# First layer's loads reordered, the last butterfly stage made as two products per tile, and a token table with 16 words per place

## The reference

```python
sim = einsum('bhnd,bhmd->bnm', Q, K) / (sqrt(d) * H)      # Q, K from the context
threshold = top_k(sim, 153)[0][:, :, -1:]
A = sigmoid(sim) * (sim >= threshold)
A = (A + swapaxes(A, -1, -2)) * 0.5
x = x + tanh(g_xattn[0]) * ((1 - gamma) * layernorm(x) + gamma * A)

hidden = silu(up_gate) * up_lin                            # (b, s, 2048)
hidden = fwht(hidden)                                      # 11 butterfly stages, / sqrt(2048)
x = x + tanh(g_ffn[0]) * einsum('bsh,dh->bsd', hidden, W2)
```

```python
topk_vals, topk_idx = top_k(xf @ router_w.T, 2)
order = argsort(topk_idx.reshape(-1))
x_sorted = xf[order // 2]
```

## Time and profile before

| what | us |
|---|---|
| median of 3 runs | 3995.62 |
| profiled execution, its own time | 4001.03 |
| its span (first to last instruction) | 3999.2 |
| PE busy | 3661.6 (92%) |
| DVE busy | 1982.6 (50%) |
| ACT busy | 1377.6 (34%) |
| POOL busy | 355.7 (9%) |

### The profile page before, as it was taken

How to read it: one execution, slowest core, us unless ns; L and a number is a source line. 1 busy time by engine, 2 the same in 40 slices (tenths; PEclk the granted TensorE clock), 3 DMA queues, 4 the chain that set the end, 5 groups by cost and what they waited for, 6 DMA issues and landing times.

```text
span 3999.2 us, 35714 instructions
## 1 busy us (share of the span) xinstructions
PE 3661.6 (92%) x11789; PEld 1695.6 (42%) x11790; DVE 1982.6 (50%) x3587; ACT 1377.6 (34%) x2838; POOL 355.7 (9%) x380
## 2 busy tenths in 40 slices
PE   1999999986789999599879999999999999999999
PEld 0444444432445444356534444444444434444443
DVE  8556666145678776211156756656565652111111
ACT  5524242011357667122233443434343441100100
POOL 7000000000123231211111100000000000000000
PEclk6999999998889999799989999999999999999999
DMA  3321312300322322455532101010101102222221
GB/s 119 126 79 54 132 57 75 112 23 22 86 69 62 74 59 82 156 162 160 170 133 67 50 32 36 24 36 24 36 24 36 36 1 84 85 78 79 84 84 52
DMA packets 78347, 295.90 MB, mean 74 GB/s; under 512 B 10856, under 2 KB 11752, under 8 KB 66684
## 3 DMA queue, kind: packets, MB, share of 16 engines
q1 hardware_dynamic: 69856, 268.35, 21.0%
q0 software_dynamic: 8352, 25.78, 2.1%
HBM read 255.73 MB, written 33.64 MB: 72 GB/s over the span
## 4 chain that ended last, share of the span: by engine, by line
PE 79%; DVE 8%; issue 7%; ACT 3%; DMA 2%; POOL 1%; SPq 0%; DVEq 0%; POOLq 0%; ACTq 0%
PE BM L2293 6%; PE BM L2348 5%; PE BM L529 5%; PE BR L529 5%; PE BR L2357 4%; PE BM L364 4%; PE BR L364 4%; PE BS L2331 3%; PE BS L545 3%; PE BT L545 3%; PE BT L2340 3%; PE BM L2306 3%; PE BR L1989 3%; PE BM L1978 2%; PE BR L1978 2%
## 5 line engine op out<-in xcount | busy, mean ns | idle before, releaser
L2422 ACT ACTIVATE AR<-BS,AR 128x512 f32<-128x512 f32 x256 | 174.5, 685 | 411.5 <-DVE AR L2517 411.5
L2416 ACT COPY AR<-BM 128x512 f32<-128x512 f32 x340 | 198.8, 585 | 307.2 <-PE BM L2348 99.9
L2530 DVE SCALAR_TENSOR_TENSOR X<-BR,AR,X 128x512 f32<-128x512 f32 x256 | 191.9, 750 | 206.2 <-PE BR L2357 197.1
L2517 DVE TENSOR_REDUCE AR<-BS 128x2 f32<-128x1024 f32 x128 | 156.9, 1226 | 253.8 <-PE BS L2331 253.8
L2357 PE MATMUL BR<-AR 128*128 128x512 f32 x512 | 254.8, 621 | 4.2 <-DVE X L2530 0.6
L2348 PE MATMUL BM<-AR 128*128 128x512 f32 x512 | 246.7, 594 | 0.0
L2293 PE MATMUL BM<-XT,AR 128*128 128x512 f32 x512 | 236.6, 605 | 0.7 <-ACT XT L239 0.7
L364 PE MATMUL BM<-XT,AR 128*128 (+1 forms) x512 | 231.7, 595 | 4.9 <-DMA AR<-l_w_dram 4.9
L419 DVE TENSOR_TENSOR AR<-AR,BR 128x512 f32<-128x512 f32 x64 | 44.0, 688 | 379.5 <-PE BR L364 379.5
L529 PE MATMUL BM<-XT,AR 128*128 128x512 f32 x512 | 230.6, 593 | 0.9 <-ACT AR L632 0.9
L529 PE MATMUL BR<-XT,AR 128*128 128x512 f32 x512 | 230.2, 592 | 0.0
(11 more groups left out here) (383 smaller groups left out, 5919.0 us busy)
## 6 DMA issues: line engine op xcount, KB each, us to landing
AR<-l_w_dram SPq DMA_DIRECT2D x128, 512.0 KB, 3.5
AR<-l_wq_dram SPq DMA_DIRECT2D x32, 1152.0 KB, 5.2
AR<-l_w_dram SPq DMA_DIRECT2D x42, 768.0 KB, 4.9
AR<-w2h SPq DMA_DIRECT2D x16, 1024.0 KB, 4.8
QS<-qx SPq DMA_DIRECT2D x32, 512.0 KB, 10.0
AR<-l_w_dram SPq DMA_DIRECT2D x16, 1024.0 KB, 4.8
AR<-l_w_dram SPq DMA_DIRECT2D x8, 1408.0 KB
made<-AR SPq DMA_DIRECT2D x40, 256.0 KB, 4.9
```

The lines of the kernel that those rows point to most:

```text
L2416: nc.scalar.copy(to, BM[:, L3[job] % 2, :]).then_inc(m_free, 1)
L2530: nc.vector.scalar_tensor_tensor(out=xb, in0=BR[:, L3[job] % 2, :], scalar=RS3[:, p % 2, h, st:st + 1], in1=xb, op0=ALU.mult, op1=ALU.add) ...
```

## The change

Five things change. (1) SyncE issues the first batch's context, the two projection weights and `HAD` first; TensorE waits for these four alone, the wait for `loaded` (now four loads) moves to VectorE, to `turn_graph` and to ScalarE behind its projection copies. The rest of the context is a load of its own behind `W2`; GpSimd and TensorE wait for it (`x_rest`) before they use it. ScalarE's wait for VectorE's first step in the first batch is gone. (2) `had_pool` makes three stages instead of four, and begins only behind VectorE's additions of the first batch. (3) The fourth stage is made by TensorE: each rotated tile is the sum of two products, with `HAD` and with `HAD` or its negative `NHAD`, which ScalarE makes at the start. (4) Ten of the sixteen tiles are made ahead of `turn_graph`; ScalarE takes five of them between the last five rounds of the search. (5) The table of tokens has 16 words per place, so that words lie 64 B apart; it is cleared by one store of 8192 pieces of 128 B, indices are scaled by 16, and `SLT` is gathered with all 16 words per place.

The diff, cut to its core:

```diff
 TW = NT + 2
+APART = 16
 EK = 3
...
         WH = [a(HID // P, D), a(HID // P, D)]
+        NHAD = a(P)
         TRIAL_I, DROP_I, DROP_P = TRIAL.bitcast(I32), DROP.bitcast(I32), BS[:, 0, 0:ST].bitcast(I32)
...
             pool.wait_ge(l0f.m.full, 2 + ST + HAD_M)
+            pool.wait_ge(x_rest, 32)
             nc.gpsimd.tensor_copy(KXH.bitcast(F32R), CT).then_inc(kx_hi, 1)
...
-            pool.wait_ge(l0_had, 32)
+            pool.wait_ge(l0_had, 16)
+            pool.wait_ge(vec, ADD_NORM)
             n = 0
-            for stage in range(4):
+            for stage in range(HAD_STAGES):
                 w = 1 << stage
-                of, to = WH[stage % 2], WH[1 - stage % 2]
+                of, to = WH[1 - stage % 2], WH[stage % 2]
                 of = of.rearrange("p (g two w) d -> p g two (w d)", two=2, w=w)
...
         HAD_M = HID // P
+        HAD_STAGES, HAD_EARLY, HAD_BETWEEN, ADD_NORM = 3, 10, 5, 2 + ST
         NU = B * ST * UG
...
-            pe.wait_ge(l0_w, 32)
+            def last_butterfly(t):
+                bank, half = start_job(pe, f.m, m), HAD_M // 2
+                nc.tensor.matmul(bank, HAD, WH[0][:, t % half, :], start=True, stop=False)
+                nc.tensor.matmul(bank, HAD if t < half else NHAD, WH[0][:, t % half + half, :], start=False, stop=True)\
+                  .then_inc(f.m.full, 1)
+
+            pe.wait_ge(l0_w, 64)
             project(0)
             similarities()
+            pe.wait_ge(butterflies, 2 * HAD_STAGES)
+            for t in range(HAD_EARLY):
+                last_butterfly(t)
+            pe.wait_ge(loaded, 64)
             turn_graph(0)
-            pe.wait_ge(butterflies, 8)
-            for t in range(HAD_M):
-                nc.tensor.matmul(start_job(pe, f.m, m), HAD, WH[0][:, t, :], start=True, stop=True).then_inc(f.m.full, 1)
+            for t in range(HAD_EARLY, HAD_M):
+                last_butterfly(t)
             N_PE.step()
             norm_tensor(pe)
+            pe.wait_ge(x_rest, 32)
             pe.wait_ge(turn.free, T_PE.now() + 2)
...
             def similarities(b):
-                act.wait_ge(graph_ready, b * ST + 1)
+                if b:
+                    act.wait_ge(graph_ready, b * ST + 1)
                 for st in range(ST):
...
+            def take_hadamard(t):
+                nc.scalar.activation(WH[1][:, t, :], full(act, f.m, m), ACT.Copy, scale=float(HID ** -0.5)).then_inc(f.m.free, 1)
+
+            act.wait_ge(l0_w, 64)
+            nc.scalar.activation(NHAD, HAD, ACT.Copy, scale=-1.0)
             project()
+            act.wait_ge(loaded, 64)
+            nc.scalar.activation(G[:, :], G[:, :], ACT.Tanh).then_inc(g_ready, 1)
+            nc.scalar.activation(GC[:, 0:1], GC[:, 0:1], ACT.Sigmoid).then_inc(g_ready, 1)
             similarities(0)
-            count(BITS)
+            count(BITS - HAD_BETWEEN)
+            for t in range(HAD_BETWEEN):
+                take_hadamard(t)
+                count(1)
             tr.step()
-            for t in range(HAD_M):
-                nc.scalar.activation(WH[1][:, t, :], full(act, f.m, m), ACT.Copy, scale=float(HID ** -0.5)).then_inc(f.m.free, 1)
+            for t in range(HAD_BETWEEN, HAD_M):
+                take_hadamard(t)
             norm_scalar(act, 0)
...
             norm_turned(0)
-            v.wait_ge(x_rest, 16)
+            v.wait_ge(x_rest, 32)
             for b in range(B):
...
         xnd = nc.dram_tensor("xnd", [B * S, D], F32, kind="Internal").ap()
-        table = nc.dram_tensor("table", [P * P, 1], F32, kind="Internal").ap()
+        table = nc.dram_tensor("table", [P * P * APART, 1], F32, kind="Internal").ap()
         ROUTE_AT = AREA - 848
...
             link(v, nc.vector.tensor_reduce(POS, EQ, op=ALU.add, axis=AX.X))
-            nc.vector.tensor_copy(idx[:, b * ST:(b + 1) * ST], POS).then_inc(idx_ready, 1)
+            nc.vector.tensor_scalar(idx[:, b * ST:(b + 1) * ST], POS, float(APART), None, ALU.mult).then_inc(idx_ready, 1)
             v.wait_ge(idx_ready, 2 * b + (1 if idx is IDX0 else 2))
...
             nc.gpsimd.memset(ONE, 1.0).then_inc(ones_ready, 1)
-            pool.wait_ge(table_zero, 64)
+            pool.wait_ge(table_zero, 16)
             pool.wait_ge(l2_in, 80)
...
         ROW = a(1).bitcast(I32)
-        SLT = a(P)
+        SLT = a(P, APART)
         IX = [a(1).bitcast(I32) for _ in range(2)]
...
             pe.wait_ge(slt_in, 16)
-            nc.tensor.transpose(start_job(pe, er, r)[:, 0:P], SLT, ID[:, :]).then_inc(er.full, 1)
+            nc.tensor.transpose(start_job(pe, er, r)[:, 0:P], SLT[:, :, 0], ID[:, :]).then_inc(er.full, 1)
             pe.wait_ge(turn.free, T_PE.now() + 2)
...
             for idx, yp in ((IDX0, YP0), (IDX1, YP1)):
-                link(v, nc.vector.tensor_scalar(SHIFTED, idx, 11, None, ALU.arith_shift_right))
+                link(v, nc.vector.tensor_scalar(SHIFTED, idx, 15, None, ALU.arith_shift_right))
                 link(v, nc.vector.tensor_copy(AT_E, SHIFTED))
...
                 link(v, nc.vector.tensor_reduce(AT_E, OFFS, op=ALU.add, axis=AX.X))
-                link(v, tt(AT_E, AT_E, idx, ALU.add))
+                link(v, nc.vector.scalar_tensor_tensor(out=AT_E, in0=idx, scalar=1.0 / APART, in1=AT_E, op0=ALU.mult, op1=ALU.add))
                 link(v, nc.vector.tensor_scalar(yp, AT_E, float(P), None, ALU.add))
...
             pool.wait_ge(table_in, 2 * B * ST * 16)
-            nc.gpsimd.indirect_dma_start(out=SLT, out_offset=None, in_=table.rearrange("(r n) o -> r (n o)", n=P),
+            nc.gpsimd.indirect_dma_start(out=SLT.rearrange("p n a -> p (n a)"), out_offset=None, in_=table.rearrange("(r n) o -> r (n o)", n=P * APART),
                                          in_offset=bass.IndirectOffsetOnAxis(ap=ROW, axis=0)).then_inc(slt_in, 16)
...
             x_tiles = x.rearrange("(n p) d -> p n d", p=P)
+            sp.dma_start(CT[:, 0:S], ctx_t[:, 0:S]).then_inc(l0_w, 16)
+            sp.dma_start(WQ0, l0_wq).then_inc(l0_w, 16)
+            sp.dma_start(WK0, l0_wk).then_inc(l0_w, 16)
+            sp.dma_start(HAD, hadamard).then_inc(l0_w, 16)
             sp.dma_start(X[:, 0:ST, :], x_tiles[:, 0:ST, :]).then_inc(loaded, 16)
-            sp.dma_start(CT, ctx_t).then_inc(loaded, 16)
             sp.dma_start(ID[:, :], ident).then_inc(loaded, 16)
...
             sp.dma_start(GC[:, 0:1], gamma_raw.rearrange("(a n) -> a n", a=1).to_broadcast([P, 1])).then_inc(loaded, 16)
-            sp.dma_start(WQ0, l0_wq).then_inc(l0_w, 16)
-            sp.dma_start(WK0, l0_wk).then_inc(l0_w, 16)
-            sp.dma_start(HAD, hadamard).then_inc(l0_had, 16)
-            sp.dma_start(WH[0], l0_w2).then_inc(l0_had, 16)
+            sp.dma_start(WH[1], l0_w2).then_inc(l0_had, 16)
+            sp.dma_start(CT[:, S:], ctx_t[:, S:]).then_inc(x_rest, 16)
             sp.dma_start(X[:, ST:, :], x_tiles[:, ST:, :]).then_inc(x_rest, 16)
             sp.wait_ge(zero_ready, 1)
-            for c in range(4):
-                sp.dma_start(table.rearrange("(p n) o -> p (n o)", p=P)[:, 32 * c:32 * c + 32], ZERO[:, :]).then_inc(table_zero, 16)
+            sp.dma_start(table.rearrange("(p a n) o -> p a (n o)", p=P, n=32),
+                         ZERO[:, :].rearrange("p (o n) -> p o n", o=1).to_broadcast([P, P * APART // 32, 32])).then_inc(table_zero, 16)
             l0_sync(sp)
...
         def _(pe):
-            pe.wait_ge(loaded, 80)
             l0_tensor(pe)
...
             act.sem_inc(turn.free, 2)
-            act.wait_ge(loaded, 80)
-            nc.scalar.activation(G[:, :], G[:, :], ACT.Tanh).then_inc(g_ready, 1)
-            nc.scalar.activation(GC[:, 0:1], GC[:, 0:1], ACT.Sigmoid).then_inc(g_ready, 1)
             l0_scalar(act)
...
         def _(v):
-            v.wait_ge(loaded, 80)
+            v.wait_ge(loaded, 64)
             norm_vector(v, 0)
```

## The result

The changed kernel takes 3966.19 us (median of four runs, 3964.13 to 3966.96) against 3994.91 for the kernel before beside it: ratio 0.9927, interval 0.9910 to 0.9944, so 28.7 us less. The profiled execution spans 3965.1 us against 3999.2.

The account below looks back on a forecast made before the run. TensorE, busy 92% of the span, bounds the kernel; the change shortens two of its waits. First layer 10.2 plus table 6.0 makes 16.2 us off the median 3995.62: 3979.4, range 3974.5 to 3991.

Parts of the forecast that it names:

- the part on the table: At the router: spaced words gain 8.2 us, the larger gather loses 2.2, net 6.0; bounds 2.2 lost and 9.0 gained.
- the last scatter then lands as other transfers do: At the router: the last scatter's 12.4 us becomes 4.2, between 3.4 and 4.9, if its tail goes.
- the larger gather: At the router: fetching 1 MB instead of 64 KB takes 5.6 us instead of 3.4, a loss of 2.2.
- The loads: At the start: projections start 5 us earlier, the search 3.8 us earlier; the first layer in all gains 10.2 us.
- Rival 4: At the start: loads land no earlier (11.8 for the gates), nearly 3 us lost, 3982.4; chance 0.60 together with the forecast.
- VectorE's start: At the start: the last load VectorE waits for lands at 9.0 us, between 8.0 and 11.8.
- The step behind the search: VectorE's L766 after the top-k search no longer waits for GpSimd: 6.41 falls to 0.16 us.
- the first rotated tile: In the search, behind round 27: ScalarE waits 4 us for TensorE's tile, which comes at 76.0.
- rival 3: Early tiles inside the search: TensorE's clock stays low, a tile costs 3.76 instead of 1.72, 4010.0 us; chance 0.06.
- The zeroing: In SP's queue: 8192 pieces take 2.5 to 24 us, end by 54, up weights by 60; counted as nothing.
- Rivals 1 and 2: At the router: the tail stays, 3987.6 us, chance 0.23; or spacing makes it worse, 10.5 us doubling, 3998.1, chance 0.08.

Follow-up runs that it names:

- e4_no_early: The kernel before without the scatters of the first three batches, whose tokens the table then lacks: 3988.68 us, ratio 0.9977.
- e2_loads_only: The changed kernel with one word per place (APART = 1, the old table) and the shift to match, keeping its changed first layer: 3989.21 us, ratio 0.9979.
- e5_apart2: The changed kernel with 2 words per place instead of 16, words 8 bytes apart: 3967.18 us, ratio 0.9923.
- e1_table_only: The kernel before with only the table's part of the change (16 words per place, index, shift, zeroing, gather): 3975.20 us, ratio 0.9943.
- e3_apart4: The changed kernel with 4 words per place instead of 16, words 16 bytes apart: 3964.35 us, ratio 0.9915.

## Why the prediction was wrong

**The step that failed.** In the part on the table the forecast counted one scatter: "the last scatter then lands as other transfers do", a gain of 8.2 us, net 6.0. The table's change alone is worth 22.8 us. At the place it looked at, the mechanism was right and the sizes near: from the last scatter to the gather 10.2 us went (8.2 forecast), the larger gather cost 2.3 (2.2 forecast), net 7.9. What was put at nothing is the same scatters in earlier batches, where the late report that costs is not the scatter's own, for which nobody waits, but that of the copies of maxima, for which TensorE waits. In their place the runs show a third layer 13.3 us shorter with the spaced table alone. It is the first two batches that cost: the third one's scatters, from 1589.36 on in the kernel before, lie behind the last copy at 1586.0. The trace of before had it: 12.3 us of waits on that small copy in the page's fifth part, of which 3.3 remain, and 10.52 us in the chain for 8 KB. I had read the chain only where the scatter itself was waited for.

The Trainium skill, DMA: Bandwidth & Descriptors, section Queues, rings and completion order, says that a semaphore's increment by a DMA lands only after every earlier write of that DMA engine, in whatever queue. The trace agrees: a copy on SyncE's queue reports 10.52 us after its issue behind GpSimd's scatters, more than 7 us after its queue's last packet, and TensorE's waits of this kind fall to 3.4 us with the scatters gone (e4_no_early). That this order of writes is what holds the report is argued: no run shows which of the 16 DMA engines held it, or where.

**The loads.** Forecast 10.2 us, measured 8.9 at the first stream and 8.7 in the time (e2_loads_only; 4.8 to 12.0 by its interval). The projections started at 5.38 (near 5.8 forecast). Rival 4 came true in part: the last of the small loads, gamma, was in at 11.0 instead of 9.0 (11.8 in the rival), GpSimd began at 21.17 instead of 19.0 and ended at 74.42 instead of 72.2, and this reached the end, partly: the search ended at 89.2 (87.6 forecast), the graph was turned by 96.39 (95.2), the six late tiles done at 106.7 (105.5). The mis-sized term is VectorE's start, with 2.1 us, of which 1.3 reached the long stream. Neither of the two other orders tried brought the four loads in earlier than this one did at its best (10.0, e5_apart2).

**What held.** The step behind the search fell to 0.16 us. ScalarE waited 5.12 us for the first rotated tile (about 4 forecast). The clock rose on the way, against rival 3; windows of the changed kernel, as the earlier trace rows:

```profile
76.00:78.00 2.00, 2.00 (x3) 0.67 (x2) 0.00 (x0) 0.00 (x0) 0.00 (x0) 0.50 0.00 0
78.00:80.00 2.00, 2.00 (x4) 0.91 (x3) 0.00 (x0) 1.72 (x4) 0.00 (x0) 0.54 0.00 0
80.00:85.00 5.00, 5.00 (x13) 2.15 (x12) 3.86 (x18) 4.43 (x13) 0.00 (x0) 1.00 0.00 0
```

From 74.47, where TensorE became busy again, it was 0.50 until about 80, then 1.00; two tiles were slow, not eight. The zeroing, 30.6 us long from its issue at 6.88, was in by 37.5 (54 at the latest in the forecast); the up weights were issued behind it by 37.0, long before their first product at 111.7.

**Rivals 1 and 2** fall with e1_table_only. With them falls what I made of the Trainium skill, DMA: Bandwidth & Descriptors, section Specifications, which says that below 512 B the DMA does a read-modify-write: that a lone word would then be as dear as one beside its neighbour. Each word is still 4 bytes in e3_apart4, and GpSimd waits 1.96 us for the last scatter instead of 12.18.

**The chances.** Faster was given 0.68. The range was too narrow below because its lower end took the forecast's places as the only ones: it allowed 3.0 us more for the table, where 13.3 stood under a different name in the third layer.

## What to carry to other kernels

When a transfer's report comes late although its packets are through, look for every other DMA in flight at that time, wherever the same kind of store runs, and not only for who waits on this one: a stall appears under the name of the innocent neighbour. Where small stores to scattered places report late, try room between them; here 16 bytes were enough, and 64 only made the gather dearer. A wait of TensorE can cost more than its length: here 9.4 us of idle time went from the third layer, and 5.3 us more because fewer products ran at half clock.

## What was not expected of the hardware

The wait for a scatter of 4-byte words changes with the spacing of the table that they go to: 12.18 to 16.59 us with words 4 bytes apart, 3.53 at 8 bytes, 1.96 at 16 and at 64. Behind such scatters at 4 bytes, 8 KB copies of another queue reported 5.84 to 11.07 us after their issue where TensorE waited for them; the one it waited for ahead of the first scatter took 1.90. At the start, the last of four loads that together bring 1.1 MB beside 0.45 MB of others came at 10.0 to 11.1 us in the three orders that were run.
